# Graph layer on one core: the cross sums along r are multiplied on GpSimd between its gathers, not on VectorE, and TensorE adds them in one product of 192 columns

## The chip, the core and the metric

The kernel runs on one core of a Trainium2 chip. A core has five engines that run side by side, each with its own instruction stream: TensorE (PE in the profile; PEld is its loading of weights), VectorE (DVE), ScalarE (ACT), GpSimd (POOL) and SyncE (SP), which here only issues DMAs. They are held together by semaphores: an instruction may raise one when it ends, and an engine may wait until one has a value. The metric is the device time of one execution, in microseconds (us).

## What is computed

For each of 412,500 edges (x has 12,500 nodes of 32 features) a small network makes the weights of a tensor product of the features at both ends of the edge and the edge's direction; the results are summed by destination node. The reference, cut to what the change touches:

```python
sh1 = SQRT3 * r                                  # r: unit vector of the edge, 3 numbers
s1, v1 = ...                                     # 16 scalars, 16 vectors of 3, from both ends
w = _mlp(emb, fc1_w1, fc1_w2)                    # per edge: Wss, Wvv, Wsv, Wvs, each 16 x 8
v_t = a1 * (jnp.einsum('eu,euw->ew', s1, Wsv)[:, :, None] * sh1[:, None, :]
            + jnp.einsum('euk,euw->ewk', v1, Wvs))
...
edge_out = jnp.concatenate([jnp.tanh(scal), (vecs * jnp.tanh(gates)[:, :, None]).reshape(E, 24)], axis=1)
return jax.ops.segment_sum(edge_out * norm[:, None], edge_dst, num_segments=num_nodes)
```

The change is in `v_t`. The first einsum is the cross sum, 8 numbers per edge; times the three components of r it gives 24, which are added to the second einsum.

## The kernel before

Edges are taken in 403 super-tiles of 1024: 128 partitions of 8 edges each (G = 8; C = 8 is the width of a result). In names of tiles, t is the edge in the partition, w the result, k the component of a vector, u the summed index.

**Stages.** The work on a super-tile is spread over several passes of a loop. In the body for position `at`, `two` is the super-tile whose first layer is multiplied out, `three` the one before it (second layer), `four` the one before that (tanh, messages, sum by destination), `one` and `zero` are the next two (features taken apart, gathers), and `three_on` is further ahead. `periods` runs six bodies in the open, then a loop with two bodies to a turn, then the last ones. Each engine has its own copy of this loop and its own order in it, written by hand; only semaphores couple them. `a.n(1, 1)` is the count of a semaphore when super-tile `a` has raised it, `a.n()` the count before that, `a.n(1, -1)` one less.

**TensorE** fills one half of the PSUM tile `pw` with 128 weights per edge (`fill`, 8 matmuls, line 1038), seven times per super-tile. **VectorE** multiplies each fill with features (lines 1293, 1300, 1307, 1315, 1323, 1338 twice, 1348, 1355), and writes products to `prods`. TensorE sums products over u by transposing matmuls that accumulate in PSUM (`added`, line 1043), ScalarE copies the transposed sums out (line 813 `vs_t`, 823 `st_t`, 835 `gates_t`, 840 `osum_t`) and TensorE turns them back.

**The cross sum** isn't made on TensorE. VectorE's line 1315 (`cross_products`) makes the products, line 1331 (`cross_sum`) reduces them to `sv` [128 x 8 edges x 8]. Then come the first half of the gate products of super-tile `three` (line 1338), and line 1370 (`cross_along`): `sv` times r for each component, 192 numbers per partition, into `svr`. It reads r from `r_near`, a copy in PSUM that VectorE makes itself (line 1364). Line 1397 (vector part of the messages of `four`) and the second half of the gate products (1338) follow.

TensorE adds the two parts in `vector_sums_turned`: it turns `vs_t` back into `vs_ps` (192 columns of PSUM) and adds `svr` by a product with the identity, in two pieces of 128 and 64 columns (lines 1043, 1074, 1076, 1077). A float32 product that isn't a transposing one shows as two matmuls in the trace. ScalarE copies the result to `VT` (line 818).

**GpSimd** issues the eight gathers of source features of `zero` (line 654, 128 rows each), and between them does small products: line 588 r of `one`, 631 and 636 remainders of the edge features of `three_on`, 618 and 623 two additions for `two`, 598 the scalar part of the messages of `four` (it waits for the tanh of line 845 on ScalarE), 643 and 648 remainders of the hidden layer of `zero`, 610 the vectors of `one` times r (it waits for ScalarE's copy of the vectors, line 778). ScalarE's line 738 waits for line 631, and stands ahead of line 840 (`osum_t`) in ScalarE's stream; TensorE's lines 1124 and 1126 turn back `gates_t` and `osum_t`, line 845 takes the tanh, line 850 copies `osum`, for which VectorE's line 1387 waits.

Of the kernel before, what the change touches and what calls it, by code (L numbers as in the profile page):

```python
# [5 lines left out]
P = 128  # L6
G = 8
# [3 lines left out]
C = 8  # L11
# [11 lines left out]
ALU = mybir.AluOpType  # L23
# [8 lines left out]
def build_gnn_layer(nc, x, src, dst, emb_t, vec, weight, fc1_w1, fc1_w2, fc2_w1, fc2_w2, out):  # L32
# [63 lines left out]
    with ExitStack() as ctx:  # L96
# [7 lines left out]
        identity = sb("identity", [P, P])  # L104
        identity_bf = sb("identity_bf", [P, P], BF16)
        halves = sb("halves", [P, P // 2])
# [43 lines left out]
        r = sb("r", [P, 2, G, 3])  # L150
# [6 lines left out]
        sv = sb("sv", [P, G, C])  # L157
# [47 lines left out]
        vs_ps = p3[:, 0:3 * G * C]  # L205
# [156 lines left out]
        def wait(eng, semaphore, value):  # L362
            if isinstance(value, int) and value <= 0:
                return
            eng.wait_ge(semaphore, value)
# [196 lines left out]
        def _(pool):  # L562
# [18 lines left out]
            def directions(a):  # L581

                p = a.par
                pool.wait_ge(vec_in[p], a.k(16))
                pool.wait_ge(inv_in[p], a.k(16))
                wait(pool, r_moved, a.n(1, -1))
                wait(pool, vr_done, a.n(1, -1))
                nc.gpsimd.tensor_tensor(r[:, p, :, :], vecs[:, p, :, :],
                                        inv_near[:, p, :].unsqueeze(2).broadcast_to([P, G, 3]), ALU.mult).then_inc(r_done, 1)

            def messages_scalar(a, windows, more):

                p = a.par
                pool.wait_ge(wgt_in[p], a.k(16))
                pool.wait_ge(th_out, a.n(1, 1))
                wait(pool, scat_mm, a.n(windows, more))
                ends = msg[:, :, :].rearrange("p t (a w) -> p a t w", w=C)[:, 0:F // C + 1:F // C, :, :]
                nc.gpsimd.tensor_tensor(ends, th[:, :, :, :], late[:, p, :].unsqueeze(1).unsqueeze(3).broadcast_to(  # L598
                    [P, 2, G, C]), ALU.mult).then_inc(msg_done, 1)

            nc.gpsimd.memset(emb_stack[:, :, :], 0.0).then_inc(stacks_zero, 1)
            nc.gpsimd.memset(w1_stack[:, :], 0.0).then_inc(stacks_zero, 1)
# [43 lines left out]
            def hid_less_second(a):  # L646
                pool.wait_ge(hid_b, a.n(1, 1))
                nc.gpsimd.tensor_tensor(hid_parts[:, a.par, :, KH - H:KH], hid_rest[:, :, :],
                                        hid_parts[:, a.par, :, 3 * H:4 * H], ALU.subtract).then_inc(hid_c, 1)

            def gathers(a, side, tiles):
                p = a.par
                for t in tiles:
                    nc.gpsimd.indirect_dma_start(  # L654
                        nodes[:, p, t, side, :], None, x_rows,
                        bass.IndirectOffsetOnAxis(ap=idx[:, p, side, t:t + 1], axis=0)
                    ).then_inc(nodes_in[p][side], 16)
# [19 lines left out]
            def program(is_general):  # L677
                def body(at, i):
# [24 lines left out]
                        emb_less_second(three_on)  # L703
                    if zero is not None:
                        gathers(zero, 0, (4,))
                        hid_less_second(zero)
                        gathers(zero, 0, (5,))
                        gathers(zero, 0, (6,))
# [289 lines left out]
        def _(pe):  # L998
# [43 lines left out]
            def added(out, column, first, last):  # L1042
                return nc.tensor.matmul(out, column, identity[:, :], start=first, stop=last, is_transpose=True)  # L1043
# [22 lines left out]
            def vector_sums_turned(a):  # L1066

                pe.wait_ge(vs_t_out, a.n(1, 1))
                pe.wait_ge(r_moved, a.n(1, 1))
                wait(pe, msg_done, a.n(2, -2))  # L1070
                wait(pe, vtr_done, a.n())
                pe.wait_ge(svr_done, a.n(1, 1))
                added(vs_ps[:, 0:P], vs_t[:, 0, :], True, False)
                nc.tensor.matmul(vs_ps[:, 0:P], identity[:, :], svr[:, 0:2, :, :].rearrange("p k t w -> p (k t w)"),  # L1074
                                 start=False, stop=True)
                nc.tensor.matmul(vs_ps[:, P:P + P // 2], vs_t[:, 1, :], halves[:, :], start=True, stop=False)
                nc.tensor.matmul(vs_ps[:, P:P + P // 2], identity[:, :], svr[:, 2, :, :].rearrange("p t w -> p (t w)"),  # L1077
                                 start=False, stop=True).then_inc(vs_back, 1)

            def scalar_sums(a):  # L1080

# [143 lines left out]
        def _(dve):  # L1225
# [133 lines left out]
            def unit(a):  # L1359
                return r_near[:, a.par, :, :].rearrange("p t k -> p k t").unsqueeze(3).broadcast_to([P, 3, G, C])  # L1360
# [2 lines left out]
                dve.wait_ge(r_done, a.n(1, 1))  # L1363
                nc.vector.tensor_copy(r_near[:, a.par, :, :], r[:, a.par, :, :]).then_inc(r_moved, 1)

            def cross_along(a):
                dve.wait_ge(r_moved, a.n(1, 1))
                dve.wait_ge(sv_done, a.n(1, 1))
                wait(dve, vs_back, a.n())
                nc.vector.tensor_tensor(svr[:, :, :, :], sv[:, :, :].unsqueeze(1).broadcast_to([P, 3, G, C]),  # L1370
                                        unit(a), ALU.mult).then_inc(svr_done, 1)

            def vt_dot_first(a):
                dve.wait_ge(vt_done, a.n(1, 1))
                wait(dve, m_vd, a.n())
# [84 lines left out]
            def program(is_general):  # L1460
                def body(at, i):
# [23 lines left out]
                        cross_sum(two)  # L1485
                    if three is not None:
                        gate_products(three, 0, ring)
                    if two is not None:
                        cross_along(two)
                    if four is not None:  # L1490
                        messages_vector(four)
                    if four is not None and not is_general:
# [94 lines left out]
```

## Time and profile before

| | us |
|---|---|
| median of 3 runs | 6505.99 |
| lowest, highest run | 6491.57, 6510.45 |
| the profiled execution, its own time | 6485.43 |
| its span, first to last instruction | 6483.5 |
| mean granted TensorE clock in it | 0.977 of full speed |

| engine | busy us | share of the span | instructions |
|---|---|---|---|
| TensorE | 5938.8 | 92% | 69422 |
| VectorE | 5877.3 | 91% | 7326 |
| GpSimd | 4979.5 | 77% | 6875 |
| ScalarE | 3998.5 | 62% | 12507 |

In a timeline row the columns are: start in us from the start of the span, duration in us, engine, line of the kernel, operation, output and inputs by name, shapes, how many instructions are merged in the row (x8), and in square brackets how long the engine was idle before and what ended that. No bracket means no idle time worth showing. Two consecutive instructions of one engine can overlap by some 0.1 us, so the distance between starts, not the duration, is what an instruction takes from an engine that never rests. "issue" is time in which the engine waited for nothing the profile shows; "remote" is a releaser that the profile doesn't know. One body of the loop is counted here from one start of VectorE's line 1293 to the next.

### The profile page before, as it was taken

The numbers are of one execution on the slowest core, as the hardware profiler recorded it, in microseconds if no ns is written. First come the engines' busy times: TensorE is split into PE (matmuls) and PEld (weight loads), VectorE is DVE, ScalarE is ACT, GpSimd is POOL, SyncE is SP. The second block draws the span as 40 slices with busy tenths as digits, with TensorE's granted clock in tenths as the row PEclk, the third lists the DMA queues.
The fourth block names the chain that finished last, engine by engine and source line by source line (L and its number), as shares of the span: only waits on it lengthen the run. The fifth ranks groups of instructions, "written<-read, shape, count | busy, mean of one in ns | idle before, by whom it ended". The sixth has DMA issues, their size and how long they took to land.

```text
span 6483.5 us, 222832 instructions
## 1 busy us (share of the span) xinstructions
PE 5938.8 (92%) x69422; PEld 5751.0 (89%) x69422; DVE 5877.3 (91%) x7326; ACT 3998.5 (62%) x12507; POOL 4979.5 (77%) x6875
## 2 busy tenths in 40 slices
PE   4999999999999999999999999999999999999997
PEld 3989989989899989998999999899998988999897
DVE  7989989989999999998999999999999999999998
ACT  5666666656666666666666666666666666666664
POOL 6777778777777777787777777787787777777774
PEclk9999999999999999999999999999999999999998
DMA  5434434434444444443444444444444444444442
GB/s 140 90 85 86 90 86 89 88 82 88 87 85 91 87 86 86 89 90 84 90 85 86 88 88 86 87 91 87 90 88 85 88 87 86 87 90 87 89 87 55
DMA packets 1671120, 569.95 MB, mean 88 GB/s; under 512 B 1535146, under 2 KB 1619083, under 8 KB 1670536
## 3 DMA queue, kind: packets, MB, share of 16 engines
q1 hardware_dynamic: 1567911, 516.43, 36.1%
q0 software_dynamic: 103168, 53.03, 5.1%
q8 instruction: 19, 0.31, 0.0%
q14 instruction: 22, 0.18, 0.0%
HBM read 302.19 MB, written 7.26 MB: 48 GB/s over the span
## 4 chain that ended last, share of the span: by engine, by line
PE 59%; issue 16%; DVE 11%; another core or an unknown queue 5%; ACT 4%; POOL 3%; DVEq 1%; SPq 1%; DMA 0%; ACTq 0%; POOLq 0%
PE p L1043 31%; PE pw L1038 16%; DVE prods L1300 3%; PE p L1131 3%; PE ph L1026 2%; POOL nodes L654 2%; DVE sv L1331 2%; PE ph L1015 1%; PE p L1126 1%; ACT off_hot L870 1%; DVE prods L1338 1%; DVE prods L1348 1%; PE p L1074 1%; PE p L1077 1%
## 5 line engine op out<-in xcount | busy, mean ns | idle before, releaser
L1043 PE MATMUL p<-identity,prods 128*128 128x128 f32 x29016 | 3599.8, 277 | 232.2 <-ACT gates_t L835 191.9
L654 POOL DMA_INDIRECT nodes<-x_rows,idx x3224 | 3104.5, 963 | 708.9 <-issue 590.1
L1043 PEld LDWEIGHTS p<-identity,prods 128*128 128x128 f32 x29016 | 3244.4, 144 | 262.4 <-issue 214.7
L1038 PE MATMUL pw<-w_stack,hid_t 128*128 128x128 bf16 x22568 | 1684.2, 221 | 176.5 <-issue 82.2
L1038 PEld LDWEIGHTS pw<-w_stack,hid_t 128*128 128x128 bf16 x22568 | 1438.2, 100 | 257.0 <-issue 111.9
L1293 DVE TENSOR_TENSOR prods<-pw,V 128x2048 f32<-128x2048 f32 x403 | 923.0, 2290 | 273.7 <-remote 175.0
L1338 DVE TENSOR_TENSOR prods<-pw,M 128x1024 f32<-128x1024 f32 x806 | 976.9, 1212 | 5.4 <-PE pw L1038 3.3
L870 ACT ACTIVATE off_hot<-node_iota,off_base 128x42 f32<-128x42 f32 x3216 | 747.0, 317 | 0.0
L1348 DVE TENSOR_TENSOR prods<-pw,VT 128x1536 f32<-128x1536 f32 x403 | 705.2, 1750 | 20.6 <-remote 18.0
L1315 DVE TENSOR_TENSOR prods<-pw,S 128x1024 f32<-128x1024 f32 x403 | 490.7, 1218 | 123.8 <-PE pw L1038 117.8
L1307 DVE TENSOR_TENSOR prods<-pw,S 128x1024 f32<-128x1024 f32 x403 | 490.8, 1218 | 14.0 <-remote 13.9
L1323 DVE TENSOR_TENSOR prods<-pw,S 128x1024 f32<-128x1024 f32 x403 | 490.9, 1218 | 9.6 <-issue 6.5
L1300 DVE TENSOR_TENSOR prods<-pw,V 128x1024 f32<-128x1024 f32 x403 | 489.2, 1214 | 0.0
L1331 DVE TENSOR_REDUCE sv<-prods 128x64 f32<-128x1024 f32 x403 | 487.5, 1210 | 0.0
L610 POOL TENSOR_TENSOR vr<-V,r 128x384 f32<-128x384 f32 x403 | 348.8, 865 | 165.8 <-issue 136.9
L845 ACT ACTIVATE th<-p 128x128 f32<-128x128 f32 x403 | 111.7, 277 | 584.5 <-PE p L1126 579.6
L598 POOL TENSOR_TENSOR msg<-th,late 128x128 f32<-128x128 f32 x403 | 164.0, 407 | 400.4 <-issue 236.6
L751 ACT ACTIVATE off_row<-dstb,row_shift 126x1024 bf16<-126x1024 int32 x403 | 459.3, 1140 | 0.1
L738 ACT ACTIVATE emb_parts<-emb_rest 80x128 bf16<-80x128 f32 x403 | 124.8, 310 | 500.6 <-POOL emb_rest L631 335.5
L757 ACT ACTIVATE hot_t<-off_row 126x1024 bf16<-126x1024 bf16 x403 | 425.2, 1055 | 0.1
L813 ACT ACTIVATE vs_t<-p 128x256 f32<-128x256 f32 x403 | 154.4, 383 | 400.4 <-PE p L1043 313.0
L801 ACT ACTIVATE hid_parts<-hid 128x768 bf16<-128x768 f32 x403 | 347.0, 861 | 0.0
(138 smaller groups left out, 8483.5 us busy)
## 6 DMA issues: line engine op xcount, KB each, us to landing
dstb<-in_dst SPq DMA_DIRECT2D x403, 504.0 KB
nodes<-x_rows,idx POOLq DMA_INDIRECT x3224
emb_stack<-emb_parts SPq DMA_DIRECT2D x2418, 20.0 KB
emb<-in_emb_t SPq DMA_DIRECT2D x403, 40.0 KB
hid_t<-hid_parts SPq DMA_TRANSPOSE x806
idx<-in_src SPq DMA_DIRECT2D x403, 4.0 KB
xw<-x SPq DMA_DIRECT2D x403, 7.9 KB
vecs<-in_vec SPq DMA_DIRECT2D x403, 12.0 KB
```

The source lines that it names most:

```text
L654: nc.gpsimd.indirect_dma_start(nodes[:, p, t, side, :], None, x_rows, bass.IndirectOffsetOnAxis(ap=idx[:, p, side, t:t + 1], axis=0)).then ...
L870: nc.scalar.activation(off_hot[:, t, :], node_iota[:, :], ACT.Square, bias=off_base[:, t:t + 1]).then_inc(off_hot_done, 1)
L1038: mm = nc.tensor.matmul(pw[:, slot, t, :], hid_t[:, layer, a.par, t, :], w2_stack[:, lo:lo + W], start=True, stop=True)
L1043: return nc.tensor.matmul(out, column, identity[:, :], start=first, stop=last, is_transpose=True)
L1293: nc.vector.tensor_tensor(prod_v01.rearrange("p u k t w -> p k t u w"), wts.unsqueeze(1).broadcast_to([P, 2, G, 2 * C, C]), V[:, p, 0:2, : ...
L1300: nc.vector.tensor_tensor(prod_v2.rearrange("p u t w -> p t u w"), wts, V[:, a.par, 2, :, :].unsqueeze(3).broadcast_to([P, G, 2 * C, C]), ...
L1307: nc.vector.tensor_tensor(prod_s[:, :, 0, :, :].rearrange("p u t w -> p t u w"), weights(a, 1, ring).rearrange("p t (u w) -> p t u w", w=C ...
L1315: nc.vector.tensor_tensor(prod_c, weights(a, 2, ring).rearrange("p t (w u) -> p t w u", w=C), S[:, a.par, :, 0:2 * C].unsqueeze(2).broadca ...
L1323: nc.vector.tensor_tensor(prod_s[:, :, 1, :, :].rearrange("p u t w -> p t u w"), weights(a, 3, ring).rearrange("p t (u w) -> p t u w", w=C ...
L1331: nc.vector.tensor_reduce(sv[:, :, :], prod_c, AX.X, ALU.add).then_inc(sv_done, 1)
L1338: nc.vector.tensor_tensor(prod_g[:, :, half, :, :].rearrange("p u t w -> p t u w"), weights(a, 4 + half, ring).rearrange("p t (u w) -> p t ...
L1348: nc.vector.tensor_tensor(prod_o[:, :, 0:3, :, :].rearrange("p u k t w -> p k t u w"), wts.unsqueeze(1).broadcast_to([P, 3, G, C, C]), VT[ ...
```

## The change

GpSimd gets a function `cross_along` with VectorE's product, reading r from its own tile in place of the copy in PSUM. It stands behind the fifth gather, ahead of `hid_less_second`. `directions`, which overwrites r, now also waits for `svr_done` of the super-tile that used the same half. VectorE's `cross_along` and its call go. TensorE adds `svr` first, in one product of 192 columns, and accumulates the turned sums on it.

```diff
@@ directions (GpSimd)
                 wait(pool, vr_done, a.n(1, -1))
+                wait(pool, svr_done, a.n(1, -1))
@@ GpSimd
+            def cross_along(a):
+                pool.wait_ge(sv_done, a.n(1, 1))
+                pool.wait_ge(r_done, a.n(1, 1))
+                wait(pool, vs_back, a.n())
+                nc.gpsimd.tensor_tensor(svr[:, :, :, :], sv[:, :, :].unsqueeze(1).broadcast_to([P, 3, G, C]),
+                                        r[:, a.par, :, :].rearrange("p t k -> p k t").unsqueeze(3).broadcast_to([P, 3, G, C]),
+                                        ALU.mult).then_inc(svr_done, 1)
@@ GpSimd's body
                         gathers(zero, 0, (4,))
+                    if two is not None:
+                        cross_along(two)
+                    if zero is not None:
                         hid_less_second(zero)
@@ vector_sums_turned (TensorE)
                 pe.wait_ge(svr_done, a.n(1, 1))
-                added(vs_ps[:, 0:P], vs_t[:, 0, :], True, False)
-                nc.tensor.matmul(vs_ps[:, 0:P], identity[:, :], svr[:, 0:2, :, :].rearrange("p k t w -> p (k t w)"),
-                                 start=False, stop=True)
-                nc.tensor.matmul(vs_ps[:, P:P + P // 2], vs_t[:, 1, :], halves[:, :], start=True, stop=False)
-                nc.tensor.matmul(vs_ps[:, P:P + P // 2], identity[:, :], svr[:, 2, :, :].rearrange("p t w -> p (t w)"),
-                                 start=False, stop=True).then_inc(vs_back, 1)
+                nc.tensor.matmul(vs_ps, identity[:, :], svr[:, :, :, :].rearrange("p k t w -> p (k t w)"),
+                                 start=True, stop=False)
+                added(vs_ps[:, 0:P], vs_t[:, 0, :], False, False)
+                nc.tensor.matmul(vs_ps[:, P:P + P // 2], vs_t[:, 1, :], halves[:, :], start=False, stop=True
+                                 ).then_inc(vs_back, 1)
@@ VectorE's body
                         gate_products(three, 0, ring)
-                    if two is not None:
-                        cross_along(two)
                     if four is not None:
                         messages_vector(four)
```

Where the instructions stand now. First GpSimd, in the body of the loop, from the message product on; before:

```order
L598 TENSOR_TENSOR msg<-th,late 128x2x8x8 [waits scat_mm,th_out,wgt_in1]
L654 DMA nodes<-x_rows,idx 128x32
L643 TENSOR_TENSOR hid_rest<-hid,hid_parts 128x256 [waits hid_c,hid_a]
L654 DMA nodes<-x_rows,idx 128x32
L636 TENSOR_TENSOR emb_parts<-emb_rest,emb_parts 80x128 [waits emb_b]
L654 DMA nodes<-x_rows,idx 128x32
L648 TENSOR_TENSOR hid_parts<-hid_rest,hid_parts 128x16x16 [waits hid_b]
L654 DMA nodes<-x_rows,idx 128x32 x2
```

and with the change:

```order
L599 TENSOR_TENSOR msg<-th,late 128x2x8x8 [waits scat_mm,th_out,wgt_in1]
L663 DMA nodes<-x_rows,idx 128x32
L652 TENSOR_TENSOR hid_rest<-hid,hid_parts 128x256 [waits hid_c,hid_a]
L663 DMA nodes<-x_rows,idx 128x32
L645 TENSOR_TENSOR emb_parts<-emb_rest,emb_parts 80x128 [waits emb_b]
L663 DMA nodes<-x_rows,idx 128x32
L606 TENSOR_TENSOR svr<-sv,r 128x192 [waits vs_back,r_done,sv_done]
L657 TENSOR_TENSOR hid_parts<-hid_rest,hid_parts 128x16x16 [waits hid_b]
L663 DMA nodes<-x_rows,idx 128x32 x2
```

The product stands as the one new row, and all behind it comes after it.

Then TensorE, in the same body, at the vector sums (`scatter` ahead of them, the next super-tile's first fill behind); before:

```order
L1131 MATMUL p<-hot,msg 32x42 x7
L1043 MATMUL p<-identity,vs_t 128x128 [waits vtr_done,msg_done,svr_done,r_moved,vs_t_out]
L1074 MATMUL p<-svr,identity 128x128
L1076 MATMUL p<-halves,vs_t 128x64
L1077 MATMUL p<-svr,identity 128x64
L1038 MATMUL pw<-w_stack,hid_t 128x128 [waits turned_in00,pgf_done]
```

and with the change:

```order
L1142 MATMUL p<-hot,msg 32x42 x7
L1085 MATMUL p<-svr,identity 128x192 [waits vtr_done,msg_done,svr_done,r_moved,vs_t_out]
L1055 MATMUL p<-identity,vs_t 128x128
L1088 MATMUL p<-halves,vs_t 128x64
L1050 MATMUL pw<-w_stack,hid_t 128x128 [waits turned_in01,pgf_done]
```

Four products have become three, behind the same waits; the one that reads `svr` is now the first.

## Rows read from the trace of the kernel before

**Rows 1.** Part 1 of the page: busy us, share and instructions of each engine.

```profile
PE 5938.8 (92%) x69422; PEld 5751.0 (89%) x69422; DVE 5877.3 (91%) x7326; ACT 3998.5 (62%) x12507; POOL 4979.5 (77%) x6875
```

**Rows 2.** View of line 1293: durations, first and last start, idle time before it.

```profile
L1293 DVE TENSOR_TENSOR prods<-pw,V x403: 2270/2292/2294, 83.5 to 6414.2; 128x2048 f32<-128x2048 f32 x135
...
  remote: 175.0, 117
  PE pw L1038: 45.9, 157
```

**Rows 3.** Timeline of VectorE: first and last row of 13 calm periods.

```profile
2747.29 2.29 DVE L1293 TENSOR_TENSOR prods<-pw,V 128x2048 f32<-128x2048 f32 x1 [0.49 <-issue]
...
2940.62 2.27 DVE L1293 TENSOR_TENSOR prods<-pw,V 128x2048 f32<-128x2048 f32 x1
```

**Rows 4.** Timeline of VectorE around line 1370.

```profile
3019.76 1.21 DVE L1331 TENSOR_REDUCE sv<-prods 128x64 f32<-128x1024 f32 x1
3020.89 1.22 DVE L1338 TENSOR_TENSOR prods<-pw,M 128x1024 f32<-128x1024 f32 x1
3022.02 0.35 DVE L1370 TENSOR_TENSOR svr<-sv,p 128x192 f32<-128x192 f32 x1
3022.28 0.42 DVE L1397 TENSOR_TENSOR msg<-p,msg 128x192 f32<-128x192 f32 x1
```

**Rows 5.** Timeline of GpSimd over one body and the start of the next.

```profile
3013.52 0.94 POOL L654 DMA_INDIRECT nodes<-x_rows,idx  x1 [0.30 <-issue]
...
3014.67 0.43 POOL L631 TENSOR_TENSOR emb_rest<-emb,emb_parts 80x128 f32<-80x128 f32 x1
...
3017.56 0.41 POOL L598 TENSOR_TENSOR msg<-th,late 128x128 f32<-128x128 f32 x1 [0.42 <-issue]
...
3022.58 0.69 POOL L648 TENSOR_TENSOR hid_parts<-hid_rest,hid_parts 128x256 bf16<-128x256 f32 x1
...
3026.08 0.86 POOL L610 TENSOR_TENSOR vr<-V,r 128x384 f32<-128x384 f32 x1 [0.46 <-issue]
...
3028.38 0.95 POOL L654 DMA_INDIRECT nodes<-x_rows,idx  x1 [0.30 <-issue]
...
3029.53 0.43 POOL L631 TENSOR_TENSOR emb_rest<-emb,emb_parts 80x128 f32<-80x128 f32 x1
```

**Rows 6.** Timeline of TensorE at the vector sums of the same body.

```profile
3023.48 0.33 PE L1043 MATMUL p<-identity,vs_t 128*128 128x128 f32 x1
3023.65 0.39 PE L1074 MATMUL p<-svr,identity 128*128 128x128 f32 x2
3023.87 0.33 PE L1076 MATMUL p<-halves,vs_t 128*128 128x64 f32 x2
3024.04 0.39 PE L1077 MATMUL p<-svr,identity 128*128 128x64 f32 x2
3024.26 0.61 PE L1038 MATMUL pw<-w_stack,hid_t 128*128 128x128 bf16 x8
```

**Rows 7.** Timeline of three engines: marks in two bodies that follow each other.

```profile
2997.08 2.29 DVE L1293 TENSOR_TENSOR prods<-pw,V 128x2048 f32<-128x2048 f32 x1 [0.49 <-issue]
2999.19 0.44 POOL L631 TENSOR_TENSOR emb_rest<-emb,emb_parts 80x128 f32<-80x128 f32 x1
3002.04 0.28 ACT L845 ACTIVATE th<-p 128x128 f32<-128x128 f32 x1 [1.69 <-PE p L1126]
3003.22 0.35 DVE L1387 TENSOR_TENSOR p<-osum,p 128x192 f32<-128x192 f32 x1
3011.64 2.29 DVE L1293 TENSOR_TENSOR prods<-pw,V 128x2048 f32<-128x2048 f32 x1
3017.15 0.28 ACT L845 ACTIVATE th<-p 128x128 f32<-128x128 f32 x1 [1.32 <-PE p L1126]
3018.01 0.36 DVE L1387 TENSOR_TENSOR p<-osum,p 128x192 f32<-128x192 f32 x1
3026.54 2.29 DVE L1293 TENSOR_TENSOR prods<-pw,V 128x2048 f32<-128x2048 f32 x1 [0.41 <-PE pw L1038]
```

More of the change, by code:

```diff
@@ L1364, in bring_directions @@
                 nc.vector.tensor_copy(r_near[:, a.par, :, :], r[:, a.par, :, :]).then_inc(r_moved, 1)
[L1366 to L1371, printed above, removed]
             def vt_dot_first(a):
```

## The prediction

> **What bounds the kernel now.** I read the first part of the page first, then the distances between the starts of one instruction, then single periods in the timeline. The busy shares say only that no engine is idle much: TensorE 92%, VectorE 91%, GpSimd 77% [rows 1]. VectorE's first product of a super-tile (line 1293) starts 403 times, from 83.5 to 6414.2 us [rows 2], so a mean period is (6414.2 - 83.5) / 402 = 15.75 us. A calm stretch is quicker: 13 periods from 2747.29 to 2940.62 us, 14.87 each [rows 3]. The missing 0.88 us a period, 354 us in all, lies in disturbed periods. Half of it is idle time of VectorE ahead of line 1293 whose releaser the view calls "remote" (175.0 us, 117 times [rows 2]): what the profile shows had all been done by then. I can't say what delays it. It isn't touched by the change, so I let it stay and put its chance variation into the range.
>
> So the question is what sets a calm period. Two of them, from 2997.08 to 3026.54 us [rows 7], take 29.46, or 14.73 each, and in them VectorE has just one gap, 0.41 us at the loop's end; such a gap stands at other loop turns too (0.49 before 2747.29 and 2997.08 [rows 3, 7]) and I count it as work. **VectorE's own work is therefore the longest loop: 14.73 us**, and waits of 0.14 on the average are added to it in the calm stretch.
> GpSimd's loop is found in the same way. From its first gather of a body at 3013.52 to the next at 3028.38 are 14.86 us, in which it waits 0.42 us before the message product (for tanh) and 0.46 us before line 610 (for the vectors) [rows 5]. The short gaps of 0.16 to 0.30 us ahead of each gather are there every time and go with the gather. GpSimd's own work is 14.86 - 0.88 = **13.98 us**.
>
> **What VectorE loses.** Line 1370 goes. It lasts 0.35 us, but instructions overlap: line 1370 starts at 3022.02, line 1397 at 3022.28 [rows 4]. What leaves the path is the distance, 0.26 us. The instruction ahead (1338) starts 1.13 us before 1370, and would have that distance to 1397. VectorE's loop becomes 14.73 - 0.26 = 14.47 us. Alone that would be worth 402 x 0.26 = 105 us.
>
> **What TensorE loses.** Now the four products around the sums take: line 1074, two passes of 128 columns, 3023.65 to 3023.87, 0.22 us; line 1077, two passes of 64 columns, 3024.04 to 3024.26, 0.22 us [rows 6]. One product of two passes takes their place, with 192 columns. 64 and 128 columns cost the same here, so 192 costs at least 0.22; in proportion to the 128 it would be 0.33. So 0.11 to 0.22 us is saved. The products that turn vs_t are as before; only the order changes. This isn't on VectorE's loop, and I cost it at nothing: the fill behind it is recorded from 3024.26 [rows 6], and VectorE takes it up at 3026.54 only [rows 7]. If TensorE's work set the pace it would be worth 44 to 88 us.
>
> **What GpSimd gains.** One product of 192 elements per partition. GpSimd takes 0.41 us for 128 (line 598) and 0.69 us for 256 (line 648) [rows 5]. These are the bounds; I take their middle, 0.55, since 192 lies midway and line 598 too reads broadcast operands. With 0.02 us from one instruction to the next: 0.57. It stands between the fifth gather and the second hidden subtraction. **GpSimd's loop becomes 13.98 + 0.57 = 14.55 us** (bounds 14.41 to 14.69): now the longest, just above VectorE's 14.47.
>
> A rule that speaks against the move is in the Trainium skill, "GPSIMD Engine Reference", section 4.1 "Engine selection": two-input elementwise work belongs on VectorE, GpSimd being about twice as slow. By that page twice the 0.35 us of line 1370 is 0.70, GpSimd's loop 14.70, and nearly all of the forecast's gain would be gone. The rows of GpSimd's own products give 0.55 and decide the sum.
>
> **The new waits.** GpSimd's product waits for sv_done, r_done and vs_back. The sum of line 1331 ends at 3019.76 + 1.21 = 3020.97; the slot is where line 648 now starts, behind the fifth gather, at 3022.58 [rows 4, 5]. The sum comes 1.6 us early, and r and vs_back belong to earlier times: GpSimd waits for none. TensorE in its turn wants the product when it begins the vector sums, at 3023.48 [rows 6]. Started at 3022.58, the product ends at 3023.13; with some 0.1 us for the signal 0.25 us is left. That is little, but behind TensorE's wait only the next fill and the gate sums are queued, and these have their own reserve. Cost: nothing, and 0.3 us a period if GpSimd falls 0.5 us behind. In `directions` the wait for svr_done is for a super-tile two back; nothing.
> All that stands behind the product on GpSimd moves by up to 0.57 us: the second hidden subtraction (its transposes start many us later), three gathers, then line 610, whose 0.46 us of waiting absorbs most, then the direction, line 631, and the message product, with 0.42 us of waiting. Both waits are nearly used up: 0.88 - 0.57 = 0.31 us, less the 0.26 by which VectorE's period would fall. SyncE's load of indices, which waits for the eighth gather's landing, moves with it; no one waits for that within a period.
>
> **The sum.** The longest loop falls from 14.73 (VectorE) to 14.55 (GpSimd), by 0.18. Not all of this arrives. Before, the next loop was 0.75 us shorter than the longest; after, two are within 0.1 us, and each late signal now costs one or the other. I take 0.22 us of waits in place of 0.14, so 14.77 against 14.87: 0.10 us a period, 402 x 0.10 = **40 us**. The profiled execution took 6485.4 us (span 6483.5 and 1.9 around it), 20.6 us less than the median of the runs, 6506. So 6445 for such an execution, and 6466 for a median; I say 6465.
>
> **Rivals.**
> *GpSimd's lateness goes round through ScalarE and TensorE (slower).* ScalarE can't copy the output sums out until GpSimd's line 631 has ended, and TensorE's turn of them, and the tanh, follow. In the body from 2997.08 line 631 ended at 2.55 us after line 1293, the tanh at 5.24, and line 1387 started at 6.14; in the body from 3011.64 these were 3.46, 5.79 and 6.37, and that period was 14.90 against 14.56 [rows 7]. After the change GpSimd would be late in every body. The way round: from the message product (3017.56) to the end of line 631 (3029.53 + 0.43) are 12.40, less the wait of 0.46, plus 0.57: 12.51. From the end of line 631 (3015.10) to the message product 2.46 [rows 5]. Sum 14.97, 0.10 above today's 14.87: +40 us, 6546. It decides as soon as the tanh depends on line 631 and not on VectorE. For it: the late bodies are the longer ones. Against: both may be late from a common cause.
> *The whole 0.26 us arrives.* GpSimd's product costs 0.41 and the waits melt away: 6506 - 105 = 6401. Against: GpSimd's loop, 14.41, with 14.47 for VectorE, leaves no room for any wait.
> *Nothing arrives.* Line 1293 was released 117 times by "remote" and 157 times by TensorE's fill [rows 2]: if these signals, and not VectorE's own work, set the start, the freed 0.26 us becomes a longer wait there. 6506.
>
> **How the numbers follow.** The forecast 40%, the way round 30%, nothing 20%, the whole 10%. Of the forecast's 40, 33 are faster by over 0.3% (20 us, about what a measurement of this kernel can tell from no change) and 7 are within it; the whole gives 10 faster; of nothing 15 are within and 5 slower; of the way round 27 are slower and 3 within. Faster 0.43, same 0.25, slower 0.32. The range takes in the whole gain (6401) and the way round (6546), each with some 20 us for the disturbed periods, which can come more or less often: 6385 to 6565.
>
> **What would show it.** Right: in calm stretches a period near 14.75; GpSimd's wait before the message product and before the vector product near zero, GpSimd's busy share above 80%; its new product 0.5 to 0.6 us; a gap on VectorE somewhere before line 1293 or the q product. The way round: the tanh later than 5.8 us after VectorE's first product in nearly every body, and calm periods near 15. The whole: calm periods of 14.5 to 14.6. Wrong altogether: TensorE waiting for GpSimd's product, or a share of disturbed periods unlike before, which alone could move the time by tens of us.

## The result: 2.9% slower, and the loss lies where the prediction had looked away

The changed kernel takes 6684.7 us (median of 4 runs, 6656.1 to 6731.9), the kernel before beside it 6498.8 us (4 runs, 6481.8 to 6510.5). The ratio is 1.0295, with a 95% interval of 1.0258 to 1.0332. The ratios here and below are the ones on record, estimated from all fast runs of both kernels; they can differ from the quotient of the two medians by up to 0.25%. The prediction was 6465 us, faster, with a range up to 6565. It was wrong in its sign and in its range.

First the same view as [rows 1], of the kernel after: part 1 of the page.

```profile
PE 5965.3 (89%) x68616; PEld 5801.2 (87%) x68616; DVE 5792.7 (87%) x6923; ACT 3982.9 (60%) x12507; POOL 5184.4 (78%) x7278
```

The work moved as planned: VectorE has 403 instructions less and is 84.6 us less busy, GpSimd has 403 more and is 204.9 us busier. The moved product in the timeline of GpSimd, after (start, duration, engine and line, operation, operands):

```profile
3051.09 0.95 POOL L663 DMA_INDIRECT nodes<-x_rows,idx  x1 [0.16 <-issue]
3052.06 0.56 POOL L606 TENSOR_TENSOR svr<-sv,r 128x192 f32<-128x192 f32 x1
3052.55 0.68 POOL L657 TENSOR_TENSOR hid_parts<-hid_rest,hid_parts 128x256 bf16<-128x256 f32 x1
```

It lasts 0.56 us and takes 0.49 of GpSimd's time. The view of that line shows who waited (ns minimum, median, maximum of one; then us, times):

```profile
L606 POOL TENSOR_TENSOR svr<-sv,r x403: 541/547/560, 100.4 to 6624.2; 128x192 f32<-128x192 f32 x135
its engine sat idle before it (us, times) until:
  DVE sv L1342: 7.2, 2
who waited for it (us, times):
  PE p L1085: 1.6, 6
```

So neither GpSimd's new wait nor TensorE's costs anything. TensorE's sums in the same body, after, to be held against [rows 6]:

```profile
3053.28 0.59 PE L1085 MATMUL p<-svr,identity 128*128 128x192 f32 x2
3053.70 0.27 PE L1055 MATMUL p<-identity,vs_t 128*128 128x128 f32 x1
3053.81 0.33 PE L1088 MATMUL p<-halves,vs_t 128*128 128x64 f32 x2
3053.98 0.61 PE L1050 MATMUL pw<-w_stack,hid_t 128*128 128x128 bf16 x8
```

From the first of these products to the fill behind them are 0.70 us (3053.28 to 3053.98), where the same sums took 0.78 (3023.48 to 3024.26).

Where is the loss, then? VectorE's first product of a body (line 1293 before, 1304 now, compare [rows 2]) starts from 83.2 to 6615.0 us, a mean period of 16.25 us against 15.75. The periods under 15.3 us became shorter, 14.57 on the average in place of 14.81, and fewer, 191 in place of 243. Those over 16.5 us went from 92 to 154. The loss is all in these: what they hold above 14.7 us each grew from 328 to 593 us, and all other periods together gave some 65 us back.

A long period is seen best at ScalarE's copy of the turned gate sums, gates_t (line 835 before, 847 after), for which TensorE waits. First the view of its line before the change:

```profile
L835 ACT ACTIVATE gates_t<-p x403: 272/277/278, 122.3 to 6437.9; 128x128 f32<-128x128 f32 x135
its engine sat idle before it (us, times) until:
  remote: 235.8, 87
  PE p L1043: 130.6, 210
...
who waited for it (us, times):
  PE p L1043: 191.9, 87
```

And after it:

```profile
L847 ACT ACTIVATE gates_t<-p x403: 277/277/282, 122.0 to 6638.6; 128x128 f32<-128x128 f32 x135
its engine sat idle before it (us, times) until:
  remote: 506.6, 133
  PE p L1055: 216.0, 269
who waited for it (us, times):
  PE p L1055: 402.9, 146
```

TensorE waits 211 us more for gates_t (402.9 less 191.9), and the execution is 202 us longer (spans 6685.8 and 6483.5). gates_t in its turn waits for "remote": TensorE's recorded sums had all ended (their ends are modelled by the profile, and not measured). One such body of the kernel after, TensorE first:

```profile
3020.44 1.92 PE L1055 MATMUL p<-identity,prods 128*128 128x128 f32 x16
3022.20 0.61 PE L1050 MATMUL pw<-w_stack,hid_t 128*128 128x128 bf16 x8
3022.64 0.39 PE L1104 MATMUL p<-halves,st_t 128*128 128x64 f32 x2
3026.42 0.90 PE L1055 MATMUL p<-identity,prods 128*128 128x128 f32 x3 [3.39 <-ACT gates_t L847]
```

ScalarE in the same body:

```profile
3026.09 0.28 ACT L847 ACTIVATE gates_t<-p 128x128 f32<-128x128 f32 x1 [3.95 <-remote]
```

And SyncE's queue there:

```profile
3017.76 4.89 SPq L415 DMA_DIRECT2D emb_stack<-emb_parts  x6
3022.89 1.23 SPq L426 DMA_TRANSPOSE hid_t<-hid_parts  x1
3025.22 0.61 SPq L407 DMA_DIRECT2D emb<-in_emb_t  x1
```

The sixteen sums that gates_t copies had ended by 3022.4. ScalarE starts at 3026.09, 3.7 us later, and TensorE stood still for 3.39 us. In that time SyncE had issued the transposing DMA of hid_t (line 426), at 3022.89; its completions are recorded from 3026.07 on. The semaphore that gates_t waits for is recorded at 3026.07 too, and TensorE's next two signals, of the fill (line 1050) and of the turn of st_t (line 1104), only at 3026.29 and 3026.34, while one of VectorE (3025.39) and one of GpSimd (3025.53) had come in between. So TensorE's side is late as a whole. Whether its products ended late or only its signals came late, the records don't tell; I say "late signal" for both. I come back to this.

The copy just ahead of gates_t in ScalarE's stream, VT (line 818 before, 830 after), tells the opposite story. It waits for TensorE's signal behind the vector sums. Before the change:

```profile
L818 ACT ACTIVATE VT<-p x403: 298/330/340, 110.1 to 6426.8; 128x192 f32<-128x192 f32 x135
...
  remote: 210.9, 232
```

and after it:

```profile
L830 ACT ACTIVATE VT<-p x403: 298/326/341, 109.8 to 6627.5; 128x192 f32<-128x192 f32 x135
...
  remote: 1.9, 2
```

So late signals were there before the change too, but most of them met VT, and VectorE, which needs VT, waited 2.1 us for it in all. With the change VT hardly waits, and gates_t, for which TensorE itself waits, is late more often.

### The profile page after: what moved, and what is told of

The parts are those of the page before. It is cut to its first block, busy times and chain, and to the rows that moved or that the text cites. A ratio compares the mean times of both kernels' runs of the same rounds, so it can differ in the third digit from the quotient of the medians.

```text
span 6685.8 us, 221220 instructions
## 1 busy us (share of the span) xinstructions
PE 5965.3 (89%) x68616; PEld 5801.2 (87%) x68616; DVE 5792.7 (87%) x6923; ACT 3982.9 (60%) x12507; POOL 5184.4 (78%) x7278
## 4 chain that ended last, share of the span: by engine, by line
PE 50%; issue 16%; DVE 11%; another core or an unknown queue 9%; ACT 4%; POOL 3%; SPq 3%; DVEq 1%; DMA 1%; ACTq 0%; POOLq 0%
PE p L1055 30%; PE pw L1050 11%; DVE prods L1311 2%; POOL nodes L663 2%; PE ph L1038 2%; PE ph L1027 2%; DVE prods L1349 2%; PE p L1142 2%; DVE prods L1326 1%; DVE sv L1342 1%; SPq L415 1%; PE p L1137 1%; PE p L1085 1%; DVE prods L1366 1%
## 5 line engine op out<-in xcount | busy, mean ns | idle before, releaser
L1055 PE MATMUL p<-identity,prods 128*128 128x128 f32 x29016 | 3657.5, 280 | 445.2 <-ACT gates_t L847 402.9
L1055 PEld LDWEIGHTS p<-identity,prods 128*128 128x128 f32 x29016 | 3297.0, 145 | 469.6 <-issue 343.7
L1050 PEld LDWEIGHTS pw<-w_stack,hid_t 128*128 128x128 bf16 x22568 | 1461.6, 100 | 131.4 <-DVE prods L1311 80.1
L847 ACT ACTIVATE gates_t<-p 128x128 f32<-128x128 f32 x403 | 111.7, 277 | 722.7 <-remote 506.6
L599 POOL TENSOR_TENSOR msg<-th,late 128x128 f32<-128x128 f32 x403 | 164.3, 408 | 437.8 <-issue 263.9
L619 POOL TENSOR_TENSOR vr<-V,r 128x384 f32<-128x384 f32 x403 | 348.6, 865 | 43.4 <-ACT V L790 14.8
```

The lines of the kernel that those rows point to most:

```text
L1050: mm = nc.tensor.matmul(pw[:, slot, t, :], hid_t[:, layer, a.par, t, :], w2_stack[:, lo:lo + W], start=True, stop=True)
```

## The experiments

**The chips differ.** The kernel before took 6479 to 6502 us (medians) in four comparisons, the first (its chip isn't on record) and three on three different chips, and 6060 to 6062 on two others. I call the first kind late chips and the second prompt chips, for a reason that the profiles below give. Each of these chips was used for one set of runs only, so a property of the chip can't be told from one of the hour. One execution of 31 of the kernel before on a prompt chip took 6478 us; its granted clock was 0.850, against 0.972 to 0.983 in executions of that kernel on late chips, so it needn't be the same condition. Each number has to be read with the kernel before of its own chip. The kernel after, as it is, never met a prompt one.

### The parts of the change, on a prompt chip

e1 is the kernel before with TensorE's new form alone.

```
-  added(vs_ps[:, 0:P], vs_t[:, 0, :], True, False)
-  matmul(vs_ps[:, 0:P], identity, svr[:, 0:2])  ...  matmul(vs_ps[:, P:], identity, svr[:, 2])
+  matmul(vs_ps, identity, svr[:, :])
+  added(vs_ps[:, 0:P], vs_t[:, 0, :], False, False)
```

> The kernel before with only TensorE's part of the change: svr still made by VectorE, but added first, in one product of 192 columns. Theory 1 (GpSimd's longer loop costs the time): no loss, 6440 to 6510 us. Theory 2 (TensorE's new order of the products brings the late completion signals): about the time of the changed kernel, 6600 to 6700 us. Theory 3 (a shorter VectorE runs into the signals at a worse moment): as before, 6480 to 6510 us.

e2 is the kernel after with TensorE's four old products (the same diff, the other way).

> The changed kernel with TensorE's four products as they were; svr is made by GpSimd. Theory 1: the changed kernel's time, 6650 to 6750 us. Theory 2: the loss is gone, 6400 to 6520 us. Theory 3: 6650 to 6750 us.

e3 is the kernel after, in which VectorE makes a spare product at the old place, and TensorE waits for it too:

```
 VectorE:  +  if two is not None:
           +      spare_product(two)
 TensorE:  +  pe.wait_ge(spare_done, a.n(1, 1))
```

> The changed kernel, in which VectorE also makes a product of the same shape at its old place, into a tile that nobody reads (TensorE waits for it too, since it reads the PSUM bank that the vector sums write). Theory 1: nothing regained, 6680 to 6800 us. Theory 2: 6680 to 6800 us. Theory 3: near the kernel before, 6480 to 6560 us.

e4 is the kernel before, in which GpSimd makes a spare product, which nobody reads, at the new place (VectorE's cross sum then also waits until that product of the last turn is done):

```
   gathers(zero, 0, (4,))
+  if two is not None:
+      spare_product(two)
   hid_less_second(zero)
```

> The kernel before, in which GpSimd makes the same product as well, at its new place, into a tile that nobody reads. Theory 1: the loss appears without anything else, 6620 to 6750 us. Theories 2 and 3: as before, 6480 to 6530 us.

| kernel | median us | ratio to before (6061.6) | 95% interval |
|---|---|---|---|
| e1, TensorE's form alone | 6060.1 | 0.9997 | 0.9988 to 1.0007 |
| e2, after with the old form | 6068.0 | 1.0010 | 1.0000 to 1.0020 |
| e3, after, VectorE keeps a product | 6065.3 | 1.0005 | 0.9996 to 1.0015 |
| e4, before, GpSimd has one more | 6066.7 | 1.0008 | 0.9998 to 1.0018 |

The three theories are that TensorE's new form, VectorE's shorter loop or GpSimd's longer one brings the loss. None of them shows here: 0.5 us more on GpSimd, or 0.26 less on VectorE, moves nothing by more than 0.1%. Something else sets the pace. SyncE's queue in one body of e1 (a row of several like instructions has their count behind the x):

```profile
3012.19 4.90 SPq L415 DMA_DIRECT2D emb_stack<-emb_parts  x6
3017.30 1.26 SPq L426 DMA_TRANSPOSE hid_t<-hid_parts  x1
3018.77 0.86 SPq L407 DMA_DIRECT2D emb<-in_emb_t  x1
3019.83 0.36 SPq L434 DMA_DIRECT2D idx<-in_src  x1
3021.16 0.39 SPq L442 DMA_DIRECT2D dstb<-in_dst  x1
3021.75 0.33 SPq L444 DMA_DIRECT2D xw<-x  x1
3022.29 1.30 SPq L426 DMA_TRANSPOSE hid_t<-hid_parts  x1
3023.79 0.48 SPq L467 DMA_DIRECT2D vecs<-in_vec  x1
...
3026.35 4.89 SPq L415 DMA_DIRECT2D emb_stack<-emb_parts  x6
```

The rows of this queue show no waits, in any run; they show that seventeen issues, one behind the other, fill 14.16 us here, and 14.70 is e1's mean period. SyncE's own waits stand in the views of waits of the two kernels, first e1 on the prompt chip (us in total, times, longest):

```profile
SPq L497 <- DVE msg L1396: 55.9, 162, 0.4
...
SPq L434 <- DMA nodes<-x_rows,idx: 6.1, 4, 1.9
```

then the kernel before, as it ran for the prediction:

```profile
SPq L444 <- PE ph L1026: 257.5, 125, 4.3
SPq L434 <- DMA nodes<-x_rows,idx: 83.4, 115, 2.5
```

On the prompt chip the waits of the loop come to less than 0.2 us a body, so the queue is full; on the late one it waits for others, for TensorE above all. That it is what bounds the kernel on a prompt chip rests on h3 below.

### The change again, and room on SyncE's queue, on a late chip

e5 is the kernel after once more, e6 the kernel before for its profile.

> The changed kernel as it is, beside the kernel before. In the four variants measured last, the kernel before took 6061.6 us on their chip, 438 us less than beside the changed kernel, and each variant came within 0.1% of it; their profiles show SyncE's queue issuing without a wait, 14.70 us for each body. Theory A, SyncE's queue sets the pace wherever TensorE isn't disturbed: the changed kernel takes the same as before within 0.2% (6050 to 6075 us) on such a chip, and its loss of 185 us is bound to the disturbed condition. Theory B, the change as a whole (both parts together, which no variant had) costs time of its own: 6150 us or more, a ratio of 1.015 to 1.03 on this chip too. Where this chip shows the kernel before at 6490 to 6510 us again, both give 6650 to 6730.

> The kernel before, unchanged, for a profile on this chip. Theory A: a mean period of 14.70 us, SyncE without waits of over 0.5 us in a body, TensorE's signal vs_back 0.0 us behind the end of the last matmul of its group. If the chip is one where it takes 6490 to 6510 us: a mean period of 15.75 us and vs_back 1.5 to 2 us late in nearly all bodies.

e7 (on the kernel before) and e8 (on the kernel after) move two of the seventeen issues to ScalarE:

```
 SyncE:    -  load_destinations(two, is_general)
 ScalarE:  +  load_destinations(two, is_general)
```

> Before, with the two DMAs late_dst and late_base issued by ScalarE at the start of its body in place of SyncE; nothing is left out. It takes 1.0 us of SyncE's 14.70 a body. Theory A: the next bound is VectorE's own work, 14.73 us by the trace of before, or about what SyncE had: 6030 to 6065 us, no more than 0.5% faster. Theory B (SyncE's queue only happens to be full): unchanged within 0.1%. A third possibility, that ScalarE's issues delay its row operations: 6080 us or more.

> The changed kernel with the same two DMAs moved to ScalarE; nothing is left out. Theory A: with SyncE at 13.7 us a body, VectorE at 14.47 and GpSimd at 14.55 set the pace, so the 0.1 to 0.2 us a body that the change takes from the longest loop arrives: 5960 to 6030 us, faster than both kernels and than the run before this one. Theory B: 6060 us as all the others. If it stays at 6060 while SyncE waits, another loop of about 14.7 us sets the pace.

| kernel | median us | ratio to before (6478.8) | 95% interval |
|---|---|---|---|
| e5, after | 6675.2 | 1.0291 | 1.0216 to 1.0366 |
| e7, before with room on SyncE | 6447.7 | 0.9959 | 0.9927 to 0.9991 |
| e8, after with room on SyncE | 6907.7 | 1.0639 | 1.0559 to 1.0720 |

e6 took 6482.2. e5 repeats the loss. e8 was a miss: the edit that gains 0.4% on the kernel before costs 3.5% (6907.7 / 6675.2) on the kernel after. The work that is moved is the same in both, so it can't be the work as such; it fits a matter of when things meet.

In e6 the mean period was 15.74 us, and TensorE's signal behind the vector sums (vs_back) is recorded 1.7 us at the median behind the modelled end of its last product, over 1 us in 298 of the 374 bodies that have a record of it: the second of the two outcomes expected.

### The parts on a late chip

e1, e2, e3 and the kernel after were run again as g1 to g4.

> Before, with TensorE's new form of the sums alone (one product of 192 columns), repeated in case this chip is one on which the kernel before takes 6480 to 6500 us. There, theory P (TensorE's order places its signals so that the late ones fall on gates_t): 6600 us or more, the whole loss of 196 us or most of it. Theory Q (VectorE's shorter loop) and theory R (GpSimd's longer one): 6440 to 6500. On a chip where before takes 6061: 6060 again.

> The changed kernel with TensorE's four old products. Where before takes 6480 to 6500: theory P expects 6440 to 6500, theories Q and R 6620 to 6700. Where before takes 6061: 6068 again.

> The changed kernel, with VectorE still making a product of the same size into a spare tile at the old place, TensorE waiting for both. Where before takes 6480 to 6500: theory Q (the time taken from VectorE lets it meet the late signals) expects 6450 to 6520, theories P and R 6620 to 6700. Where before takes 6061: 6065 again.

> The changed kernel itself once more, as the bracket of the three others on the same chip. Where before takes 6480 to 6500: 6650 to 6700. Where before takes 6061, on which it has not run: 6055 to 6075 if its loss belongs to the disturbed condition alone (SyncE's queue at 14.70 us a body sets the pace there), 6150 or more if both parts together cost time of their own.

| kernel | median us | ratio to before (6495.0) | 95% interval |
|---|---|---|---|
| g1, TensorE's form alone | 6468.5 | 0.9935 | 0.9902 to 0.9968 |
| g2, after with the old form | 6615.7 | 1.0162 | 1.0090 to 1.0234 |
| g3, after, VectorE keeps a product | 6672.8 | 1.0276 | 1.0214 to 1.0337 |
| g4, after | 6641.3 | 1.0248 | 1.0176 to 1.0321 |

Here the parts come apart. TensorE's form gains (g1), so theory P, that this form brings the loss, falls. Giving VectorE its time back takes nothing of the loss away (g3 against g4), so theory Q, that VectorE's shorter loop does, falls. All three kernels with the product on GpSimd are slower, as theory R has it.

### GpSimd's time, or where svr comes from

h1 is e4 again. h2 moves the spare product behind GpSimd's seventh gather. h4 takes time from GpSimd instead, by leaving vr_two out.

```
 h2:    gathers(zero, 0, (6,))                     h4:  -  if two is not None:
      +  if two is not None:                            -      along_rest(two)
      +      spare_product(two)
        along_first(one)
```

h3 is the kernel before with the edits of e1 and of e7 together.

> Before, with GpSimd also making a product of the size of svr, into a spare tile, in the slot where the changed kernel makes it; VectorE and TensorE as before. If the cause is GpSimd's own 0.5 us (theory R): 6600 to 6680 us where before takes 6480 to 6500, a ratio of 1.02 or so. If the cause is that TensorE gets svr from GpSimd instead of VectorE (theory V: another moment, another engine): 6480 to 6510, the same as before. Where before takes 6061: 6067 again.

> The same as h1_pool_too_again, but the spare product stands after GpSimd's sixth and seventh gather, ahead of vr (V times r), where it delays vr and not hid_parts. Theory R by total time: as h1 within 0.5%. If the slot counts (hid_parts, whose transpose SyncE then issues later): within 0.5% of the kernel before. Where before takes 6061: 6055 to 6075.

> Before, with the two edits that each gained where before takes 6480 to 6500: TensorE's one product of 192 columns (0.65%) and late_dst and late_base issued by ScalarE (0.4%). If they add: 6410 to 6440, a ratio of 0.989. If both act on the same wait: 6440 to 6470. If they act against each other through the places at which TensorE's signals come late, as the changed kernel did with the second edit: over 6500. Where before takes 6061: 6020 to 6060 (SyncE's queue no longer sets the pace).

> Before, with one operation of GpSimd left out (vr_two, the sum of the first two terms of the product along r, 0.46 us; the scalar messages then lack a term). The reverse dose of h1. Theory R: GpSimd's time counts at about 120 to 190 us per 0.5 us, so 6330 to 6420 where before takes 6480 to 6500. If GpSimd only hurts once its loop is fuller than 14.1 us: 6480 to 6500, unchanged. Where before takes 6061: 6055 to 6065.

The chip was a prompt one (before 6060.0), so h1, h2 and h4 answer only for that kind: 6066.9, 6064.0 and 6061.1 us, ratios of 1.0009 (1.0000 to 1.0019), 1.0004 (0.9995 to 1.0014) and 1.0001 (0.9992 to 1.0011). Half a microsecond more or less on GpSimd is worth nothing there. Whether the slot of the product or only its length counts (h2), and whether less work on GpSimd gains (h4), was asked of a late chip and has no answer. h3 is the find: **5899.6 us, a ratio of 0.9734** (0.9717 to 0.9750). Part 1 of its page:

```profile
PE 5743.8 (97%) x68616; PEld 5615.5 (95%) x68616; DVE 5809.7 (99%) x7326; ACT 3989.9 (68%) x12507; POOL 4957.7 (84%) x6875
```

With two issues less on SyncE the mean period is 14.29 us and most are 14.18. As TensorE's form alone gained nothing on a prompt chip (e1), it was SyncE's queue that held the pace there. By the busy shares VectorE, at 99%, is now the bound, with TensorE at 97% close to it. I had expected 6020 to 6060, since I still took VectorE's own work for 14.73 us. On prompt chips h3 beats all other kernels here; on a late one it wasn't run.

The question of h1 was put once more (i1), and e8 was run once more (i2).

> The run of h1_pool_too_again once more (before, and GpSimd also makes a spare product of svr's size), since there the kernel before took 6060 us and the question was of the other condition. Where before takes 6480 to 6500: theory R (GpSimd's own time) 6600 to 6680 us; theory V (the loss comes with TensorE's svr from GpSimd at another moment) 6480 to 6510. Where before takes 6061: 6067.

> The changed kernel with late_dst and late_base issued by ScalarE, once more. Where before takes 6061: SyncE's queue set the pace there, and h3_pe_form_sync_less, the same without GpSimd's product, took 5900 (14.3 us a body). With VectorE's product gone as well: 5800 to 5890 if VectorE is the next bound, 5900 to 5960 if GpSimd is, with its 14.55 us of own work by the prediction (5990 if that figure is right to the letter). Where before takes 6480 to 6500: 6870 to 6930 again.

This was a late chip, with the kernel before at 6501.9. i1 took 6654.6 us, a ratio of 1.0220 (1.0182 to 1.0258), and i2 took 6868.1, 1.0586 (1.0533 to 1.0638). (The profiled execution of i2 was the quickest of its four, 6769 us.) **i1 settles which part of the change loses**: a product on GpSimd that nobody reads costs 2.2%, with VectorE's and TensorE's instructions left as they were. Had the loss come with the moment at which TensorE gets `svr` (theory V), i1 would have taken 6480 to 6510 us. The view of gates_t in i1:

```profile
L849 ACT ACTIVATE gates_t<-p x403: 277/278/278, 120.8 to 6616.7; 128x128 f32<-128x128 f32 x135
its engine sat idle before it (us, times) until:
  remote: 483.7, 130
  PE p L1057: 229.7, 271
```

The same view of the same program on the prompt chip (h1):

```profile
L849 ACT ACTIVATE gates_t<-p x403: 277/277/278, 122.9 to 6022.0; 128x128 f32<-128x128 f32 x135
its engine sat idle before it (us, times) until:
  PE p L1057: 419.9, 403
```

There all 403 waits end with TensorE's sums themselves, and none with "remote".

### What the late signals meet

In every profile I counted how much later than in its quickest bodies gates_t starts, from the start of the scatter's sixteen products on. Summed over a profile, on late chips:

| profile | span us | sum of lateness us | bodies (of 402) over 2.5 us late |
|---|---|---|---|
| before (the first, e6) | 6483, 6480 | 304, 312 | 68, 69 |
| g1, TensorE's form | 6467 | 301 | 77 |
| e7, before with room on SyncE | 6427 | 310 | 35 |
| after (the first, e5, g4) | 6686, 6681, 6603 | 497, 535, 463 | 110, 132, 111 |
| g2, g3 | 6629, 6659 | 479, 515 | 107, 125 |
| i1, spare product on GpSimd | 6662 | 457 | 102 |
| e8, i2, after with room on SyncE | 6929, 6767 | 626, 575 | 183, 161 |

On prompt chips the sum is 12 us at most, in eight profiles, and no body is over 2.5 us late. On late ones it goes with most of the loss. Against the first profile of the kernel before, the span and the sum grow by 202 and 193 us in the kernel after, by 179 and 153 in i1, by 146 and 175 in g2, by 283 and 271 in i2. It isn't all: e8 grows by 446 and 322, and the gains of e7 (57 us) and g1 (17 us) aren't in it.

The other late signal goes the opposite way. In the four profiles on late chips without a product on GpSimd (before, e6, g1, e7) ScalarE stands idle for 184 to 277 us ahead of VT; in the eight with one (after, e5, g2, g3, g4, i1, e8, i2) for 3 to 6 us, as on prompt chips (3 us). So half a microsecond more on GpSimd doesn't bring the late signals about: it moves them from a copy that has time in hand to one that TensorE waits for.

Is it the granted clock of TensorE? It has two levels, 1.2 and 2.4 GHz. Of the bodies over 2.5 us late, 68 before and 110 after, none had the lower level when gates_t was due, so a lower clock doesn't make it late. Stretches at the lower level mostly start within 2 us of such a late copy, when TensorE has stood idle; they come to 302 us in the kernel before, 484 after and 1239 in e8. Work slowed in them is a part of the loss that the runs don't separate.

The lateness of gates_t isn't spread evenly. I call it due at its quickest time behind the scatter. In i2, of 182 bodies in which it was due in the last 0.4 us ahead of SyncE's issue of a transposing DMA, 160 were over 2.5 us late, 3.4 us at the median; of 16 due 0.4 to 0.6 us ahead none was, and of 186 due within 1 us behind the issue none. The late ones start 3.24 us behind that issue at the median, and 95% of them within 0.3 us of a recorded completion of a transpose (8% of moments taken at even distances are that near to one). In e5 the picture is the same and less clean: 104 of 179 that were due in the last 0.6 us, 1 of 138 due within 1 us behind the issue, 78% of the late ones at a completion. In h3, on a prompt chip, gates_t was due in the last 0.4 us ahead of the issue in 151 bodies and was late in none; in h1, in 17, with none late.

So much is counted. It suggests that on late chips a transposing DMA that is issued just behind TensorE's signal holds it up, and it isn't shown: no run moved the transpose against the sums with all else left alone. The kernel before speaks against it as a full account. In e6 only 5 of 106 bodies due in the last 0.4 us ahead of the issue were late, but 30 of 34 due 0.4 to 0.6 us ahead; the late starts lie 2.56 us behind the issue, and only 38% of them at a completion. And there vs_back, which is late in most bodies, is due some 2.4 us ahead of the issue.

## Why the prediction was wrong, step by step

- **The product on GpSimd, 0.55 us**: right, 0.547 us.
- **No new wait on GpSimd, 0.25 us in hand for TensorE**: right. TensorE waited for svr 1.6 us in all.
- **TensorE's saving, 0.11 to 0.22 us, costed at nothing**: the saving was over-estimated and its worth put too low for a late chip. The product of 192 columns takes 0.42 us, not 0.22 to 0.33, and the sums save 0.08 us a body, 32 us over the run; g1 gained 26.6. On a prompt chip (e1) it was worth nothing.
- **VectorE's own work is 14.73 us and the longest loop**: the first step that failed. h3 runs at 14.18 us in most periods, with VectorE making every product. Two periods with one short gap show that an engine was kept busy, not that it led, and the gap of 0.41 us counted as work wasn't work. SyncE's seventeen issues take 14.70 us a body where nothing is late, and the prediction worked out no loop for that queue. The calm stretch of 14.87 [rows 3] was near that 14.70.
- **GpSimd's loop goes from 13.98 to 14.55 us**: right as an amount. The mean period less GpSimd's waits ahead of the message product, the vector product and line 631 is 14.01 us before and 14.56 after (15.75 less 1.74, 16.25 less 1.69). Of the two waits that were to absorb it, that of the vector product did (165.8 to 43.4 us), that of the message product grew (400.4 to 437.8). As the longest loop it never acted: on a prompt chip SyncE's was longer.
- **The disturbed periods, 354 us, aren't touched by the change**: the step that cost the sign. The periods over 16.5 us went from 92 to 154, and the lateness of gates_t from 304 to 497 us; i1 shows that the product on GpSimd alone does this, with 457 us. I had no cause for them, and "no known cause" became "no effect" in the sum. The prediction's last paragraph named them as what could make it wrong, by tens of us; it was 200, and the range had 20.
- **The rival of the way round through ScalarE**: its sign was right, its mechanism isn't borne out, and that its chance of 30% went to the right side was luck. It wanted the tanh to end later than 5.8 us behind VectorE's first product in nearly every body, and calm periods near 15 us. The tanh was later than that in 226 bodies of 403, against 173 before, and in the periods under 15.3 us it came no later than before (5.52 us at the median, 5.54 before), and these periods became shorter.

The rule that such a product belongs on VectorE (the Trainium skill, "GPSIMD Engine Reference", section 4.1 "Engine selection") gave the right advice. Its reason, twice the time, isn't what decided here: the ratio measured is 0.547 to 0.35 us, 1.6, and on prompt chips the longer time cost 0.1% at most.

**What stays open.** What delays TensorE's signals at all. Why 0.5 us more on GpSimd moves the delay from vs_back to gates_t: SyncE's loads of indices wait for GpSimd's gathers (83.4 us before, 114.0 after; 93.7 in e6, 137.2 in e5), which would shift SyncE against TensorE, but no run tested it. Why signals are late in some sets of runs only. And the kernel after, as it is, on a prompt chip: e2 and e3 are within 0.1% of the kernel before there, the one without TensorE's form, the other with a product too many on VectorE.

## What to carry to other kernels

Stretches without a known cause are a term of the sum: ask what the edit shifts against them, and where they hold more time than the hoped gain, let the range reach across them. Read the rows of SyncE's queue before naming the bound: a queue that issues without a wait is a full engine, and two of its seventeen issues moved to ScalarE, with TensorE's form, gave 2.7% where signals were on time. Where an edit makes waits for an unknown releaser grow at one instruction, look whether they shrank at another: the delay may be old, and only what it meets be new. Run the kernel before on more than one chip ahead of an argument on tens of us: here the same edit cost 0.1% on one and 2.2% on another.

## What the runs showed of the hardware

- ScalarE's copy of TensorE's sums started 2.5 us and more behind its quickest time in 9% (e7) to 46% (e8) of the bodies on late chips, and in none on two others, where e1, e2, e3 and h1 are the same programs as g1, g2, g3 and i1 on late ones.
- The granted clock of TensorE was 0.996 on prompt chips (h1), and 0.977 before, 0.964 after and 0.911 in e8 on late ones. TensorE stood idle for gates_t for 191.9, 402.9 and 561.4 us in these three.
- A product of 192 columns in two passes took TensorE 0.42 us from its start to the next one's (3053.28 to 3053.70), two passes of 64 or of 128 columns 0.22 [rows 6].
- The issue of a transposing DMA lasts 1.23 to 1.30 us on SyncE's queue in the rows above, and each of the six stacked pieces takes 0.82 (4.90 / 6).
